# Attention scores over 32 rows in four banks, one split and transposition of the maxima per unit, and a new order of three engines' work

## The reference

```python
x = x + tanh(g_xattn[0]) * attention(layernorm(x), ctx, ctx)      # 16 heads of 8
x = x + tanh(g_ffn[0]) * moe(layernorm(x))                        # 8 experts, top 2, SwiGLU, hidden 256
x = x + tanh(g_xattn[1]) * bidaf(layernorm(x), ctx)
x = x + tanh(g_ffn[1]) * lora_moe(layernorm(x))                   # 8 experts, top 2, rank 64
```

## Time and profile before

| | us |
|---|---|
| runs shown: median (lowest to highest) | 508.64 (506.07 to 509.48) |
| the profiled execution's own time | 504.81 |
| its span, first to last instruction | 502.9 |
| PE busy of the span | 460.3 (92%) |
| DVE busy | 387.8 (77%) |
| ACT busy | 300.9 (60%) |
| POOL busy | 231.4 (46%) |

### The profile page before, as it was taken

One profiled execution on the slowest core, in us unless ns is written; L12 is line 12 of the kernel. 1 busy time (PEld: TensorE's weight loads), 2 busy tenths in 40 slices (PEclk: granted clock), 3 DMA queues, 4 the chain that ended last, 5 costly groups with the idle time before them and its releaser, 6 DMA issues. The chain is left out here.

```text
span 502.9 us, 14460 instructions
## 1 busy us (share of the span) xinstructions
PE 460.3 (92%) x4462; PEld 373.9 (74%) x4462; DVE 387.8 (77%) x1684; ACT 300.9 (60%) x752; POOL 231.4 (46%) x320
## 2 busy tenths in 40 slices
PE   2478999999999999889999999989999999899997
PEld 1246877777777787677887887768888877777996
DVE  4557789999899878767688568767799986677973
ACT  2377877777777775455555665475535556453653
POOL 2322155666666445547300377543687871314420
PEclk9999999999999999999999999999999999999999
DMA  8801011111111110146664344220100221000011
GB/s 232 323 12 54 14 33 34 42 37 37 37 37 33 35 53 24 44 131 187 183 178 140 106 134 118 78 68 18 27 22 22 57 71 33 11 1 1 1 43 43
DMA packets 44126, 34.60 MB, mean 69 GB/s; under 512 B 5922, under 2 KB 40098, under 8 KB 43812
## 3 DMA queue, kind: packets, MB, share of 16 engines
q1 hardware_dynamic: 28884, 20.02, 13.1%
q0 software_dynamic: 4384, 8.93, 6.3%
q10 hardware_dynamic: 10800, 4.92, 3.5%
HBM read 21.85 MB, written 11.99 MB: 67 GB/s over the span
## 5 line engine op out<-in xcount | busy, mean ns | idle before, releaser
L473 POOL DMA_INDIRECT sent<-xr,rowu x60 | 59.0, 984 | 62.2 <-DVE rowu L1038 48.1
L489 POOL DMA_INDIRECT yg<-done,gidx x64 | 65.4, 1021 | 31.5 <-issue 15.6
L1257 DVE TENSOR_TENSOR act<-sil,bank 128x256 f32<-128x256 f32 x71 | 29.8, 420 | 26.8 <-ACT sil L693 25.7
L927 DVE TENSOR_REDUCE mx<-bank 128x8 f32<-128x512 f32 x64 | 41.1, 682 | 10.3 <-PE bank L1691 9.9
L455 POOL TENSOR_TENSOR ve<-mv,half 128x4 f32<-128x4 f32 (+1 forms) x40 | 8.8, 221 | 85.9 <-DVE mv L851 83.2
L693 ACT ACTIVATE sil<-bank 128x256 f32<-128x256 f32 x71 | 27.2, 383 | 35.3 <-PE bank L1864 34.4
L1880 PE MATMUL bank<-f0w_s,aT 128*128 x284 | 44.4, 279 | 0.8 <-DVE yb L1263 0.8
L634 ACT ACTIVATE Pr<-bank 128x512 f32<-128x512 f32 x64 | 34.7, 597 | 14.3 <-PE bank L1705 14.3
L640 ACT ACTIVATE PT<-bank 128x512 f32<-128x512 f32 x64 | 37.2, 609 | 4.5 <-PE bank L1654 4.1
L1691 PE MATMUL bank<-QK 64*64 64x256 f32 x512 | 36.7, 404 | 2.9 <-ACT QK L624 2.9
L1880 PEld LDWEIGHTS bank<-f0w_s,aT 128*128 128x128 f32 x284 | 37.2, 191 | 1.9 <-issue 1.2
(11 more groups left out here) (254 smaller groups left out, 1287.7 us busy)
## 6 DMA issues: line engine op xcount, KB each, us to landing
xb<-sent SPq DMA_DIRECT2D x71, 64.0 KB
done<-yb ACTq DMA_DIRECT2D x71, 64.0 KB
cT<-ctx_t_dram SPq DMA_DIRECT2D x16, 128.0 KB
f0w_s<-f_w_dram SPq DMA_DIRECT2D x1, 2048.0 KB, 10.5
Pr<-ctx_t_dram SPq DMA_DIRECT2D x8, 256.0 KB
QK<-ctx_tok_dram SPq DMA_DIRECT2D x8, 256.0 KB
out_dram<-xs SPq DMA_DIRECT2D x8, 256.0 KB, 2.3
xs<-x_dram SPq DMA_DIRECT2D x2, 512.0 KB, 6.8
```

The costliest lines, as they stand in the source:

```text
L473: nc.gpsimd.indirect_dma_start(sent, bass.IndirectOffsetOnAxis(ap=rowu[:, s, 2 * k + c:2 * k + c + 1], axis=0), rows[:, c, :], None).then_ ...
L489: nc.gpsimd.indirect_dma_start(yg[:, s, j, :], None, done[0:NG1 * P, :] if u < UG else done, bass.IndirectOffsetOnAxis(ap=gidx[:, s, j:j + ...
L927: nc.vector.tensor_reduce(mx[:, g, :], bank[SC_BANK[g]][:].rearrange("p (m k) -> p m k", k=L), AX, ALU.max).then_inc(S("a_max"), 1)
```

## The change

In A the scores of all four groups are made at once over 32 rows (Q once, without masks, `QT[:, s]`), then come four maxima, one split, one transposition and one subtraction call a unit. All of P^T goes through bank 3, all of the router's results beside the attention's in bank 5. V is multiplied with 64 columns and copied out in two operations of 64 partitions. Q and K are made a unit sooner (u+3), with four buffers of `ctx` columns. The loops over registers on PE, ACT and DVE are gone (u = -4 to 15, all unrolled). Setting up is put later on DVE, PE runs matmuls on constants at the start (`warm`), and the groups of first statistics move (`STATS_IN`). In B the order of PE's step is another, its registers are computed a step ahead, and the wait for `b_ys` stands ahead of the third part. POOL's program changes in a memset and a load alone.

```diff
-SC_BANK, MT_BANK = (0, 1, 6, 7), (5, 2)
+SC_BANK = (0, 1, 6, 7)
...
-        wv_eo = sb("wv_eo", [P, 2, D])
-        bqs = sb("bqs", [P, 2])
+        wv_eo = sb("wv_eo", [P, 2, D // 2])
+        bqs = sb("bqs", [P, 1])
...
             def a_qs(u, s):
                 a.wait_ge(S("a_qk"), u + 1)
-                for j in range(2):
-                    nc.scalar.activation(QT[:, s, j, :], bank[4][:, 0:2 * P], ACT.Identity,
-                                         bias=bqs[:, j:j + 1], scale=cst[:, C_QM + j:C_QM + j + 1])
+                nc.scalar.activation(QT[:, s, :], bank[4][:, 0:2 * P], ACT.Identity, bias=bqs[:], scale=float(DH) ** -0.5)
...
-                nc.scalar.activation(PT[:, g, :], bank[SC_BANK[g]][:], ACT.Copy).then_inc(S("a_pts"), 1)
+                nc.scalar.activation(PT[:, g, :], bank[3][:], ACT.Copy).then_inc(S("a_pts"), 1)
```

ACT's turn after, then DVE's:

```diff
                 if has(u):
                     a_pts(u, 0)
...
+                if has(u + 3):
+                    a_xts(u + 3)
+                if has(u):
                     a_pts(u, 1)
...
                 if has(u - 2):
                     r_xts(u - 2)
                 if has(u):
                     a_pts(u, 2)
+                if has(u - 1):
+                    a_ats(u - 1)
+                if has(u + 1):
+                    a_mts(u + 1)
+                if has(u):
                     a_pts(u, 3)
                 if has(u + 1):
...
+                    for g in range(NG):
+                        a_exp(u + 1, 1 - s, g)
+                if has(u + 3):
+                    a_qs(u + 3, 1 - s)
+                    a_ks(u + 3, 1 - s)
+                if has(u - 3, E):
+                    a.wait_ge(ld_f0, 32)
+                    nc.scalar.activation(f0w12_h[:, u - 3, :], f0w12_s[:, u - 3, :], ACT.Copy).then_inc(S("w12_h"), 1)
+
+            for u in range(-4, UA):
+                it_a(u, u % 2)
```

```diff
+                if has(u + 4):
+                    wait(v, S("a_xt"), u + 3)
+                    v.wait_ge(S("ln0"), 2 + (u + 4) // 2)
+                    norm(u + 4, 2, xn[:, s], "a_ln")
+                if has(u - 2):
+                    r_ln(u - 2, s)
+                if u == -4:
+                    prepare()
+                if u == -1:
+                    sum_biases()
+                if has(u + 1):
+                    a_max(u + 1, 0)
+                    a_max(u + 1, 1)
+                if u == UT:
+                    t_blocks(0)
+                if has(u):
+                    a_vs(u, s)
+                if has(u + 1):
+                    a_max(u + 1, 2)
+                    a_max(u + 1, 3)
+                    a_split(u + 1)
+                if u in STATS_IN:
+                    for group in STATS_IN[u]:
+                        first_stats(group)
                 if has(u - 3):
                     r_pos(u - 3)
                     denominator(1, u - 3, 2)
...
                     r_keep(u - 3, 1 - s)
                     first_weight(1, u - 3, 2, 2, 1.0, kept_weight(u - 3, 0))
...
+            STATS_IN = {-3: (1,), -1: (2,), 0: (3, 4), 1: (5, 6, 7)}
```

Behind this DVE's turn has the gate of u-2 (`logits`, `largest`, `experts`), `a_x(u-1)`, `as_float`, `sums(1, u-1)`, `one_hot`, `moments(1, u-1)`, `r_mask(u-2)`, `a_rec(u)` and `a_nrm(u)`. PE's turn after and its step in B:

```diff
             def it_a(u, s):
+                if has(u + 1):
+                    a_s(u + 1, 1 - s)
                 if has(u):
                     a_pt(u, s, 0)
...
+                    a_v(u, s)
                 if has(u - 3):
                     r_rank(u - 3)
+                if has(u + 3):
+                    a_xt(u + 3, 1 - s)
                 if has(u):
...
+                    a_pt(u, s, 1)
                 if has(u - 2):
                     r_x(u - 2, s)
                 if has(u):
                     a_pt(u, s, 2)
+                if has(u - 1):
+                    a_at(u - 1)
+                if u == -1:
+                    warm(8)
+                if has(u + 1):
+                    a_mt(u + 1)
+                if has(u):
                     a_pt(u, s, 3)
+                if has(u + 1):
+                    a_less(u + 1)
+                if has(u - 2):
+                    r_lg(u - 2)
+                if u == UT + 1:
+                    t_row(0)
+                if has(u + 3):
+                    a_qk(u + 3, 1 - s)
...
                 if has(u - 1):
                     a_y(u - 1)
...
+                for g in range(NG):
+                    if has(u):
+                        a_pv(u, s, g)
```

```diff
+                if wide:
+                    e = chosen_by[t - 1] = expert(t, 1)
...
+                    pe.wait_ge(S("b_xts"), t)
+                    mm(bank[1 - k][:], xbh[:, 1 - k, :], high, start=True, stop=False)
                 if last >= 0:
                     pe.wait_ge(ld_b[q % 4], (t - q % 4) * 4 + 16)
...
+                if first >= 1 and last >= 0:
+                    pe.compute_val(expert(t + 1, 1))
+                if wide:
+                    mm(bank[1 - k][:], xbh[:, 1 - k, :], low, start=False, stop=False)
+                    pe.wait_ge(S("b_xls"), t)
+                if last >= 0:
+                    transposes("b_xt", bank[4], lambda c: xb[:, q % 4, :], 1)
+                if first >= 4:
+                    pe.wait_ge(S("b_ys"), t - 3)
...
+                if wide:
+                    mm(bank[1 - k][:], xbl[:, 1 - k, :], high, start=False, stop=True).then_inc(S("b_hg"), 1)
                 if first >= 3:
...
                     for j in range(2):
                         last_mm = mm(bank[2][:, 0:D], aT[:, 1 - k, j, :],
...
+                if first >= 2 and last >= -2:
+                    pe.wait_ge(S("b_act"), t - 1)
+                    transposes("b_at", bank[6], lambda c: act[:, k, P * c:P * (c + 1)], 2)
```

377 lines of the change are left out of this document (160 added, 217 removed).

## The result

The changed kernel takes **546.92 us** in the median of four runs (546.27 to 547.04), the kernel before beside it 508.13 (506.07 to 509.48): a ratio of **1.0794** (95% interval 1.0764 to 1.0824), slower by 38.8 us. The forecast was 517.1 in a range of 504 to 526: right in sign, and the chain that it names is there, but the measured time lies outside the range, and some 16 us of it come from something that the forecast has no term for. The profiled execution has a span of 544.7 us, 41.8 over before. In all that follows a ratio and its interval leave out the executions of a slower state of the chip (over 1.5% above the fastest of the same kernel, at a lower clock), while a time is the median of all of them.

A forecast was written before the change was run, and what follows sets the result against it. PE bounds the kernel before, 98% busy in A and B; a DVE-POOL circle takes over A. A +13.0, B -1.5 and -3.0 give +8.5 on 504.8, or 513.3; with 3.8 for the median, 517.1 us, range 504 to 526.

The forecast's parts named there:

- The chain that takes over: In A, r_ln to rowu on DVE, then POOL, then the next r_ln: turns at least 13.1, later 11.9 us.
- A, to the `r_ln` of B's step 0: Start, eight turns of 13.1 and four of 11.9 bring this r_ln from 206.09 to 219.1: +13.0 us.
- casts of B, first to last: B gets shorter: 1.5 us in steps 0 to 7 and 3.0 us over steps 8 to 61.
- The circle's size: In A, DVE's 4.9 us plus POOL's 8.2 in turns 4 to 11, or 7.0 in turns 12 to 15.
- says of POOL only that its order stays: In A, POOL runs rowu, four sends, w12_low and root as before, 8.1 us from rowu to root.
- PE's saving: In A, about 2.1 of PE's 11 us a turn goes, certain to become PE's idle time.
- The start: First division of A at about 34 instead of 40.0, some 6 us sooner, bounds no gain and 11.
- `warm` at "some 2 us": Constant matmuls at the start would take some 2 us out of the first three turns, by the skill's page.
- PE's busy share in A "about 70%": Sign that the forecast is right: PE's busy share in A falls from 98% to about 70%.
- The circle through `b_ys`: In B, third part, silu, product, copy and release of PE close at 1.54 us, steps at 1.58 to 1.6.
- The rival of 10.6 a turn: In A, the chain through PE bounds if r_ln is not late: 10.6 us a turn, 492 in all; chance 13%.

The follow-up runs named there:

- e2: Changed kernel with 12 constant matmuls on PE in each of two places a turn, ahead of the transpositions of xr and of the maxima: 532.09 us, 1.0523.
- e9: Changed kernel with ACT's f0w12_h cast at its turn's head, 12 + 12 constant matmuls a turn, and POOL's w12_low ahead of the four sends: 529.09 us, 1.043.
- e11: As e10, with 8 constant matmuls a turn on PE ahead of the transposition of xr: 517.19 us, 1.0192.
- e17: As e16, with only pos, own, sum and rowu of DVE's group left ahead of r_ln, the rest behind the split: 501.38 us, 0.9929.
- e15: Changed kernel with ACT's f0w12_h cast at its turn's head and 12 + 12 constant matmuls a turn, without the warm calls: 530.53 us, 1.0496.
- e4: Changed kernel with PE's wait for b_ys in B moved back behind the third part of the product: 544.83 us, 1.0683.
- e8: Changed kernel with PE's whole block step in B as in the kernel before: 541.76 us, 1.072.
- e12: Kernel before with only PE's block step in B taken from the changed kernel: 509.93 us, 1.006.
- e10: Changed kernel with rowu ahead of r_ln, ACT's cast at the head, PE's old B step, projection and logits earlier in A, more warm calls: 562.56 us.
- e13: As e11, with a_at and projection earlier, logits back behind the subtraction, and 6 constant matmuls a turn (10 in turns 0 and 1): 508.16 us, 1.0036.
- e16: As e13, with POOL's w12_low ahead of the four sends: 505.51 us, 0.9955.

## Why the prediction was right in sign and wrong in size

The sum in the prediction is +8.5 on the profiled execution; measured are +42.0 (546.84 - 504.81), of which 41.8 lie in the span. By the traces, in us over the kernel before:

| | forecast | changed kernel | `e2`, full clock |
|---|---|---|---|
| A, to the `r_ln` of B's step 0 | +13.0 | +36.2 | +20.6 |
| casts of B, first to last | -4.5 | +3.1 | +2.2 |
| the rest | 0 | +2.4 | +2.9 |

- **The chain that takes over: right, and shown.** Its signs are there in `e2`, where the clock is full: `r_ln` waits for POOL's root in turns 4 to 11 (0.8 to 2.6 us) and for the DMA in 12 to 15, POOL is idle 5.2 ahead of its first send, and the turn is 13.4, a little more than the 13.0 that PE with its constants needs in `e9`. In the changed kernel itself only every second turn waits so. With `rowu` ahead of `r_ln` and the cast at the head (`e11` to `e17`) the wait is gone.
- **The circle's size was short by 7.6** (20.6 against 13.0). `r_ln` of turn 3 is at 58.1 (57.3 forecast). The turn behind it is 15.3 instead of 13.1: POOL waited 1.76 for the cast of `f0w_h`. The next seven are 13.42 instead of 13.1, since `r_ln` to the end of `rowu` takes 5.06 and not 4.9 and POOL's part 8.2 to 8.5 and not 8.2. (The prediction's own parts of DVE's way add up to 5.06, not to the 5.0 that it gives. V's two copies, 0.84 and not 0.66, are made up for by the others.) The last four are 12.5, not 11.9: the 5.06 again, and from `rowu` to the landing 6.9 to 7.8 instead of 7.0. Beside these sizes the step that failed is the one that says of POOL only that its order stays: of a wait for ACT (the cast at the end of the turn) nothing was asked, though the diff moves it.
- **The clock: 15.6 us of A, and no term at all.** The prediction says "It is certain that PE's saving is not seen in them: it becomes PE's idle time", and leaves it there. That step failed: PE's idle time was not free here. With it the clock comes down, and then P V, on the way to the next division, takes 3.6 instead of 2.05; with the idle time filled (`e2`) the 15.6 are gone. They include what the cast for `w12_low` costs more at the lower clock, which no run took apart. The prediction did weigh the Trainium skill's page "TensorE: Matmul & The Clock Gate", but only its Part 1 on a cold start, for `warm`, which `e15` shows to be worth nothing here. The same page has, in "HAM oscillation — how this bites in real kernels", the rule that was needed: groups of matmuls with waits between them can start cold each time. The traces agree, with 0.73 to 0.80 granted over A in the changed kernel and 1.00 with constants in the gaps; the page's case has a wait for a DMA ahead of every group, here the waits are for DVE, 2.3 us at the longest.
- **The start: right.** First division at 33.9 (34 forecast). `warm` at "some 2 us" was in no term of the sum.
- **PE's busy share in A "about 70%": wrong.** It is 84 to 87%, because the same work takes longer at the lower level.
- **B: the sign failed, 7.6 us.** "The new order takes register work out of the way, so that steps of 1.7 can come down": the steps 8 to 61 went up from a mean of 1.655 to 1.698 (2.3 us more instead of 3.0 less), and steps 0 to 7 took 0.8 more instead of 1.5 less. The circle through `b_ys` was seen, but at 1.54 instead of 1.62: from the third part to the silu it has 0.53 and not 0.43. Behind it stands a circle that the prediction does not have, through ACT's copy `aT`, at 1.59 (`e4`). `e8` and `e12` put the price of the new step at 3.2 us in both kernels.
- **The rest, 2.4**, is behind B, where nothing changed: the granted clock from 380 to 400 is 0.91, and in the same place of before (340 to 360) 1.00. Runs of the kernel before differ in the same way among themselves (spans of 502.7 at a clock of 1.000 and 505.5 at 0.993).
- **The rival of 10.6 a turn** is out even with the circle cut. The best turn of the loop is 11.17, and before had 11.45. By the timeline of `e17`, with one round of softmax a unit all four maxima, V and the split lie on one way between P V and the next subtraction; that two rounds let DVE and PE work beside each other is my reading, which no run tried. `e17` gains 4.5 us in the whole, and its first division is 4.2 earlier than that of before: the start is nearly all of the gain. In none of these orders do PE's 2 us a turn buy more than the 0.3 between 11.45 and 11.17.

## What to carry to other kernels

Once an engine's work shrinks, look for what closes the turn instead, and follow *every* circle through the other engines: behind the first one cut here stood a second (a cast put at the end of a turn), and in B likewise (a copy that ACT makes in time in one order and not in another). PE's idle time has a price of its own when its later work lies on the longest way; before you give PE slack, ask where its gaps will stand, and try a few matmuls on constants in them as a test: if the kernel gets faster with more work, the clock is the loss.

## What the runs showed that I had not expected

- **Useless matmuls pay.** 24 in a turn took the changed kernel from 1.0794 to 1.0523, 8 took `e10` (553.3 to 575.8) to `e11` (514.5 to 521.9).
- **POOL's `w12_low` holds DVE, whole operations long.** In the kernel before, already, DVE's `dif`, 0.16 elsewhere, ends with it (105.37 and 105.34):

```profile
104.05 1.32 DVE L975 TENSOR_TENSOR dif<-top 128x2 f32<-128x2 f32 x1
```

```profile
104.06 1.28 POOL L498 TENSOR_TENSOR f0w_s<-f0w_s,f0w_h  x1
```

  The same befell `xn` (1.58), `xr` (1.58) and `idf` (1.40) in the kernels above, never the maxima (0.69 at most), which read a bank of PSUM. The Trainium skill says so in "SBUF — State Buffer", section "SBUF: two separate sides": DVE and GpSimd share a pair of ports under an exclusive lock (for a DVE operation in one of its two-port modes or with two inputs in SBUF), and the loser is blocked for the other's whole instruction. The traces agree; where it is on the longest way it costs 0.43 a turn (11.86 in `e13`, 11.43 in `e16`).
- **The order of the same products has a price, but not on PE alone.** A step of B takes 1.47 in the old order and mostly 1.59 in the new one (`e4`), where PE looks full in both. That it is PE's own time, or the change between two kinds of numbers, does not fit the traces: the new order has steps of 1.48 too, where ACT's copy `aT` has been ready for 0.5 us. A gap can hide in the loads of the weights, so look at PEld as well before calling an engine full.
